# A selective scan hands its finished groups over through ScalarE, GpSimd and TensorE, and two expert layers expand their first pair of slots earlier

## The reference, cut to what matters

```python
x = L0_attn_a_hidden
x = x + _L0_attn_a_ref(_layernorm(x, axis=-1), ...)   # state space layer, 4 heads
x = x + _L0_ffn_ref(_layernorm(x, axis=-1), ...)      # 16 experts, top 1, and a shared one
x = x + _L0_attn_b_ref(_layernorm(x, axis=-1), ...)   # the selective scan
x = x + _L0_ffn_ref(_layernorm(x, axis=-1), ...)      # the experts again

# _L0_attn_b_ref: D_INNER = 256, D_STATE = 16
def step(h, inp):
    dt_t, u_t, B_t, C_t = inp
    dA = jnp.exp(dt_t[..., None] * A)
    h = dA * h + (dt_t * u_t)[..., None] * B_t[:, None, :]
    y_t = jnp.einsum('bds,bs->bd', h, C_t)
    return (h, y_t)
y = y + u_c * D
y = y * jax.nn.silu(z)
out = jnp.einsum('bld,ed->ble', y, W_out)
```

## Time and profile before

| | |
|---|---|
| time, median of 3 runs | 578.69 us (577.18 to 580.83) |
| the profiled execution's own time | 577.94 us |
| its span, first to last instruction | 576.6 us |
| TensorE's mean granted clock | 0.928 of full |
| busy: PE / PEld / DVE / ACT / POOL | 475.7 / 272.6 / 424.5 / 308.6 / 311.1 us |
| instructions | 7377 |
| scan, first L1284 to last L1290 | 247.7 to 488.8 us |
| experts' first transpose, t = 0 and t = 1 | 179.6 and 517.5 us |

### The profile page before, as it was taken

How to read it: one execution, slowest core, us unless ns; L and a number is a source line. 1 busy time by engine, 2 the same in 40 slices (tenths; PEclk the granted TensorE clock), 3 DMA queues, 4 the chain that set the end, 5 groups by cost and what they waited for, 6 DMA issues and landing times.

```text
span 576.6 us, 7377 instructions
## 1 busy us (share of the span) xinstructions
PE 475.7 (82%) x2096; PEld 272.6 (47%) x2096; DVE 424.5 (74%) x865; ACT 308.6 (54%) x598; POOL 311.1 (54%) x292
## 2 busy tenths in 40 slices
PE   0994878899878999898888988797588676899995
PEld 0742445566546985362233433243234231459973
DVE  4278967586652425599999899999999999563333
ACT  2564366464462644567667765875475542444521
POOL 1029743252552226256788668895889566331155
PEclk9997898697978999989998998988988998988999
DMA  8999930000004421355565453555554451024323
GB/s 303 398 331 323 327 109 1 1 2 20 23 33 133 121 78 42 79 151 138 161 152 144 131 134 116 152 174 136 146 148 126 148 152 28 19 63 121 107 69 91
DMA packets 39992, 73.95 MB, mean 128 GB/s; under 512 B 4368, under 2 KB 20240, under 8 KB 39184
## 3 DMA queue, kind: packets, MB, share of 16 engines
q1 hardware_dynamic: 35024, 66.74, 38.7%
q0 software_dynamic: 2048, 4.20, 2.6%
q10 hardware_dynamic: 2880, 2.55, 1.4%
HBM read 66.00 MB, written 26.28 MB: 160 GB/s over the span
## 4 chain that ended last, share of the span: by engine, by line
PE 35%; DVE 28%; issue 17%; ACT 9%; POOL 6%; DMA 3%; ACTq 2%; SPq 0%; DVEq 0%; POOLq 0%
DVE arena L1290 11%; PE psum L677 6%; PE psum L729 5%; PE psum L857 4%; DVE psum L1284 3%; POOL arena L1847 2%; PE psum L741 2%; POOL arena L1801 2%; ACT L1370 2%; PE psum L776 2%; DVE stats L928 2%; PE psum L507 1%; PE psum L855 1%; PE psum L690 1%; DMA x<-x_in 1%
## 5 line engine op out<-in xcount | busy, mean ns | idle before, releaser
L1847 POOL TENSOR_TENSOR arena<-arena 128x512 f32<-128x512 f32 x127 | 158.2, 1271 | 63.8 <-DVE arena L1290 63.6
L857 PE MATMUL psum<-arena,w 128*128 128x512 f32 x256 | 139.1, 655 | 31.1 <-POOL arena L1847 28.5
L1290 DVE TENSOR_TENSOR_SCAN arena<-arena,psum 128x512 f32<-128x512 f32 x128 | 148.4, 1199 | 2.7 <-issue 2.7
L1667 ACT ACTIVATE arena<-arena 128x510 f32<-128x510 f32 x128 | 87.7, 714 | 51.4 <-DVE arena L1290 49.1
L857 PEld LDWEIGHTS psum<-arena,w 128*128 128x128 f32 x256 | 45.3, 200 | 109.9 <-POOL arena L1847 88.8
L1284 DVE TENSOR_TENSOR psum<-psum,arena 128x512 f32<-128x512 f32 x128 | 81.4, 680 | 0.1
L1732 POOL TENSOR_TENSOR arena<-arena 128x512 f32<-128x512 f32 x16 | 20.3, 1266 | 76.1 <-DVE arena L989 76.1
L677 PE MATMUL psum<-xnt,w 128*128 128x512 f32 x128 | 61.3, 628 | 0.0
L1801 POOL DMA_INDIRECT arena<-by_expert,routes x32 | 30.8, 963 | 35.6 <-DMA by_expert<-arena 20.0
L1370 ACT ACT_TABLE_LOAD x27 | 34.6, 1283 | 9.1 <-DMA c<-c_in 8.6
L1764 POOL DMA_INDIRECT by_expert<-xn,routes x32 | 32.0, 1000 | 13.5 <-issue 7.6
(11 more groups left out here) (188 smaller groups left out, 806.7 us busy)
## 6 DMA issues: line engine op xcount, KB each, us to landing
arena<-bc_store SPq DMA_DIRECT2D x64, 512.0 KB, 4.8
by_expert<-w_in SPq DMA_DIRECT2D x4, 4096.0 KB, 44.3
w<-w_in SPq DMA_DIRECT2D x1, 4427.5 KB, 13.2
arena<-by_expert SPq DMA_DIRECT2D x54, 64.0 KB, 1.9
by_expert<-arena SPq DMA_DIRECT2D x52, 64.0 KB, 1.6
by_expert<-w_in SPq DMA_DIRECT2D x1, 1984.0 KB, 67.8
x<-x_in SPq DMA_DIRECT2D x4, 256.0 KB, 7.4
out<-x SPq DMA_DIRECT2D x4, 256.0 KB, 2.7
```

What stands on the lines that cost most here:

```text
L857: nc.tensor.matmul(bank(6 + c), ident, state[c][s % 3], start=False, stop=(n == DS - 1)).then_inc(*summed.inc((s, c)))
L1290: nc.vector.tensor_tensor_scan(state[c][s % 3], decay_b[c][s % 2], bank(2 + c), 0.0, ALU.mult, ALU.add).then_inc(*state_ready.inc((s, c)))
L1667: nc.scalar.activation(live, seq, ACT.Exp, scale=a_neg[:, DS * c + n:DS * c + n + 1]).then_inc(*decay_ready.inc((s, c)))
L1847: nc.gpsimd.tensor_tensor(state[c][s % 3], state[c][s % 3], bc_row[s % len(bc_row)][:, 1, :], ALU.mult).then_inc(*y_done.inc((s, c)))
```

## The change

It has three parts; nothing that is computed changes.

1. For the groups g = 0, 1, 2 ScalarE copies both sums out of the banks in step 16 g + 17 ("sums", into the part of `dtu` that this group no longer needs; signal `sums_taken`), and GpSimd multiplies them by the gate in steps +1 and +2, one half each. `add_up` of the next group's first step now waits for `sums_taken`.
2. For these groups TensorE puts x into the bank of `project_out` by a matmul with the identity, ahead of the projection, so that ScalarE's plain copy of that bank (step +5, "add") is the new x. VectorE's measuring moves from step +5 to +6, root and scale from +6 to +7. Group 3 is closed on VectorE as before (`gate_last`, `close_last`).
3. In both expert layers `expand(0)` and `gate_slots(0)` stand ahead of turning slots 4 to 7.

```diff
@@ due_in_steps
-            what = {0: ["gate"], 4: ["project_out"], 5: ["add"], 6: ["root"], 8: ["turn"], 9: ["logits"],
+            what = {0: ["sums"], 1: ["gate 0"], 2: ["gate 1"], 4: ["project_out"], 5: ["add"], 6: ["measure"], 7: ["root"], 8: ["turn"], 9: ["logits"],
@@ experts, TensorE (ScalarE alike, with gate_slots and take_slots)
                 for k in range(n_pairs + 2):
+                    if k == 0:
+                        expand(0)
                     if k % 2 == 0 and 2 * k + GB < NSLOT:
                         turn_in(2 * k + GB)
-                    if k < n_pairs:
+                    if 0 < k < n_pairs:
                         expand(k)
@@ add_up
-                            pe.wait_ge(*(gated_b[g - 1, c] if g else shared_added[0, NGRP - 1]))
+                            pe.wait_ge(*(sums_taken[g - 1, c] if g else shared_added[0, NGRP - 1]))
@@ project_out
+                    inner = g < NGRP - 1
+                    if inner:
+                        nc.tensor.matmul(b, ident, x_cols[:, group(g)], start=True, stop=True, skip_group_check=True)
@@ VectorE's loop over the steps
-                        if what == "gate":
-                            gate_sums(g)
-                        elif what == "add":
-                            add_b(g)
+                        if what == "measure":
+                            dve.wait_ge(*added_b[g])
+                            measure(3, g)
@@ ScalarE's loop over the steps
-                        if what == "root":
+                        if what == "sums":
+                            for c in range(NCH):
+                                act.wait_ge(*summed[DS * (g + 1) - 1, c])
+                                nc.scalar.activation(dtu[:, c, group(g)], bank(6 + c), ACT.Copy).then_inc(*sums_taken.inc((g, c)))
+                        elif what == "add":
+                            act.wait_ge(*out_b_made[g])
+                            nc.scalar.activation(x_cols[:, group(g)], out_bank[1, g], ACT.Copy).then_inc(*added_b.inc(g))
+                        elif what == "root":
@@ GpSimd's loop over the steps
-                    if what == "place":
+                    if what in ("gate 0", "gate 1"):
+                        c = ("gate 0", "gate 1").index(what)
+                        pool.wait_ge(*zb_ready[g])
+                        pool.wait_ge(*sums_taken[g, c])
+                        nc.gpsimd.tensor_tensor(z[:, c, group(g)], dtu[:, c, group(g)], z[:, c, group(g)], ALU.mult).then_inc(*gated_b.inc((g, c)))
+                    elif what == "place":
```

42 lines of the change are left out of this document (24 added, 18 removed).

## The result

| | before | changed |
|---|---|---|
| time, median of 22 runs each | 577.46 us (574.33 to 581.54) | 581.2 us (576.33 to 583.23) |
| ratio | | 1.0051, 95% interval 1.0030 to 1.0072 |
| scan, first drive product to last recurrence, profiled execution | 241.1 us | 248.2 us |
| experts, first turn to third expansion, t = 0 and t = 1 | 7.54 and 7.07 us | 4.83 and 4.52 us |

What follows compares the result with a forecast made beforehand. VectorE was taken to set the scan's pace and TensorE the experts'. Scan +4.7 and experts -5.1 gave -0.4 us on the median of 578.69, so 578.3 us, range 573.8 to 582.5.

Steps and rivals of the forecast that it cites:

- the scan's term: Scan: late copies at the hand-overs cost more than VectorE's saved work; groups 0 to 2 sum to +4.7 us, low end +1.0.
- the experts' term: Both expert layers: first expansion moved into the DMA wait and TensorE's clock kept up, -5.1 us.
- pile-up in TensorE's queue: Rival, scan: TensorE's lateness makes VectorE wait again at step 23; 581.1 us, or 583.8 in full; chance 0.10.
- Group 0, forecast +3.4: First hand-over: copies behind Silu and table load delay step 19's recurrence by 4.0, less 0.66 for the addition; low end +1.5.
- Group 1, forecast +2.0: Second hand-over: late copies delay step 35's second recurrence by 2.7 us, less 0.66 for the addition; low +0.2.
- 3.4 then 1.9: Hand-overs of groups 0 and 1: half 0 summed 3.4 us after the opening matmul, half 1 1.9 us later.
- the low end of 1.0: Scan's sum if TensorE runs at full rate at the hand-overs: 1.5 + 0.2 - 0.7 = +1.0 us.
- Group 2, forecast -0.7: Third hand-over: the gate's saving is lost to a larger stall in step 53; only the addition's gain is left.
- Hidden hand-over: Rival, scan: the hand-over is hidden, so VectorE's full saving counts; -6.2 us there, total 567.4; chance 0.07.
- TensorE keeps the full clock: Rival, scan hand-overs: no slow matmuls behind the pauses; scan +1.0 us, total 574.6; chance 0.12.
- the clock falls at the experts' start: Rival, experts: TensorE's clock drops despite the shorter pauses; experts only -1.8 us, total 581.6; chance 0.16.
- within 1% as forecast: Whole kernel: no difference beyond about 1% (5.8 us), chance 0.85; faster by more 0.09, slower by more 0.06.

Runs made afterwards that it cites:

- the scan's parts alone: The changed kernel without its experts' part (parts 1 and 2 of the change alone), against the kernel before: 583.89 us, ratio 1.0101.
- The kernel with TensorE kept busy: The changed kernel plus five, six and three unread matmuls while TensorE waits for the copies of groups 0, 1 and 2: 576.01 us, ratio 0.9956 to before.
- the kernel with all gates on VectorE and the later preparations: The changed kernel without part 1, with group 2's u, Silu, rows, dt and group 3's second gate half prepared later: 570.40 us, ratio 0.9844 to before.
- the experts' part alone: The kernel before with only the first pair expanded ahead of turning slots 4 to 7: 574.83 us, ratio 0.9932 to before.
- the last version: The changed kernel with early copies, later preparations and GpSimd products, and projection with what follows one step later: 572.54 us, ratio 0.9888 to before.

## Why the prediction was wrong

**The sum.** -0.4 was 4.7 - 5.1. From the rows of three profiles the scan's term is +7.1 to +8.1, from all profiles the experts' term is -4.5 by its starts and -4.1 by its ends: together +2.6 to +4.0, and measured were +2.9 (1.7 to 4.2). The mechanism of each term was right; the scan's size was not, +4.7 where +7.1 was measured. That the time still lies inside the range is no merit of the sum: the range's upper part had been left open for a pile-up in TensorE's queue and for slow starts of the experts, and the scan's larger loss came from neither.

**Group 0, forecast +3.4: right.** Its stalls are 7.18 us against 1.56 before, less 1.97 us of work that left VectorE (a third of 3.9 and 2.0): +3.65. The pause was 5.05 us where I had 5, and the recurrences came 3.8 and 5.5 us after the opening matmul, where I had 3.4 and 5.3. In the five profiles with this hand-over as in the changed kernel the stalls are 7.2 to 8.8 us (8.5 and 8.8 with groups 1 and 2 on VectorE), so +3.4 lies at the low end of what it costs.

**Group 1, forecast +2.0: this is the step that failed.** 5.39 us of stalls less 1.97 is +3.42. Opening and copies were placed right: VectorE is 1.99 us earlier here than before (its recurrence at 369.25 against 371.24), so TensorE's 376.20 is 378.19 in the old frame, and I had 378.05. But I took "3.4 then 1.9" for the halves, the slow value for the first pair only. The two recurrences were released 3.9 and 6.7 us after the opening: the slow stretch went on through both halves (granted clock 0.50 from 376.20 to 379.78 and on to 381.48). I had worked from the row of the same place, where the second pair was already faster. The second profile of the changed kernel and that of the scan's parts alone have the same pause of 6.76 us, the same slow second half, and stalls of 5.6 us. The kernel with TensorE kept busy shows that it is the clock: 1.82 us from opening to opening at this place, and 4.3 us of the scan's 7.1 come back. My forecast had the clock's share at 3.7 (4.7 less the low end of 1.0), nearly that. What is left over without it is 2.8 where the low end said 1.0: by the stalls of the three groups +2.9, +0.5 and -1.9 (+1.5, +0.2 and -0.7 forecast; the first has the 1.0 us of later copies in it), and 1.2 outside these stalls. The 1.18 us that VectorE waits for the decays of step 34 add nothing to the loss, since right behind them it waits for the sums in any case.

The length of the slow stretch doesn't follow the pause, though. With the copies early in group 0 alone, the pause at the second hand-over was 6.88 us, and the clock was back at 1.00 for the second half:

```profile
375.89 2.08 PE L859 MATMUL psum<-arena 128*128 128x512 f32 x2 [6.88 <-ACT arena L1699]
377.76 1.75 PE L861 MATMUL psum<-arena,w 128*128 128x512 f32 x2
379.35 1.02 PE L859 MATMUL psum<-arena 128*128 128x512 f32 x2
```

With group 2 on VectorE it was 6.89 us and the same (3.26 us to the second opening, then the full rate). There group 1's stalls are 4.1 and 3.9 us, +2.1 and +1.9 with the work that left VectorE: my forecast of +2.0. In the kernel with all gates on VectorE and the later preparations, a pause of 3.14 us at this place was followed by two slow halves (3.58 us to the second opening, which then took 1.92 us for its two records). So the step that failed is the length of the slow stretch. In the changed kernel's two profiles it covered both halves, and what sets its length stays open.

**Group 2, forecast -0.7: off by 0.7.** 3.03 us of stalls against 1.10, less 1.97, is 0.0. The part on the gate was right (gated on VectorE again, no difference that can be told), and so was the larger stall in step 53, 1.74 us. What I had not seen are the stalls of 0.80 and 0.49 us ahead of it. The pair at the third hand-over took 3.23 us from opening to opening (437.11 to 440.34), in the kernel before 2.24, as TensorE's timeline of before shows:

```profile
434.37 1.13 PE L855 MATMUL psum<-arena 128*128 128x512 f32 x2 [3.95 <-DVE arena L1303]
435.34 1.48 PE L857 MATMUL psum<-arena,w 128*128 128x512 f32 x2
436.61 1.91 PE L855 MATMUL psum<-arena 128*128 128x512 f32 x2
```

In the kernel with all gates on VectorE it was 3.57, with a stall of 0.58, so this is not the copies' doing alone: TensorE pauses at this place with either order (3.95 us before, 4.09 changed, 3.79 with all gates on VectorE), and how much of the pair then runs slow differs.

**The experts, forecast -5.1: right in its rows, a little high in the mean.** First turn to third expansion 4.83 and 4.52 us, where I had 4.5 for t = 1, instead of 7.54 and 7.07; the clock stayed at 1.00. The clock falls all the same in 5 of 24 starts, and at t = 1 not all of the gain reaches the end; with both it is about -4.1.

**The rivals.** "Hidden hand-over" (-6.2 in the scan) and "TensorE keeps the full clock" are excluded by the rows; "the clock falls at the experts' start" holds at one start in five; the pile-up in TensorE's queue did not happen: behind step 20 there is no stall until step 34, and VectorE's wait for L861 is all in the groups' first steps. The ratio of +0.5% is within 1% as forecast, but by a sum that was 3.3 us off, 2.4 us of it in the three terms of the scan as the first profile has them, 0.6 to 1.0 in the experts.

**What the forecast of signs would have needed.** The trace of before had pauses of 3.26 and 3.95 us at two hand-overs, and the slow stretches behind them lay differently: from the first matmul on, and from the second pair on. One of them was taken for all. A second half at the slow rate had to be in the range of each group, as a case of its own. With the measured 3.9 and 2.8 us in place of 3.4 and 1.9, group 1 comes to +3.4; with no gain in group 2 the scan's sum is +6.8 and the forecast 578.69 + 6.8 - 5.1 = 580.4. That is hindsight; nothing in the trace of before tells which of the lengths comes.

The Trainium skill (TensorE: Matmul & The Clock Gate, HAM oscillation) describes this case in general, that waits inside a loop drop the clock and the work behind them pays, and advises a loop order without such waits. The trace agrees with the advice: the same work without the first pause, early copies for group 0, is 3.8 us faster. The Trainium skill (ScalarE: Activation LUTs, What ACT_TABLE_LOAD costs) adds a drain of about 1380 ns to a switch of tables; here again it isn't seen: the load at 311.72 is followed by the copies at 313.02, 1.30 us from start to start.

## What to carry to other kernels

Before a product is taken from the engine that sets the pace, walk the queue of the engine that gets it, at the very step: a copy of 0.6 us behind a Silu and two table loads cost more than the 2 us that it saved, and the same copy ahead of them brought the scan back to its old length. A pause of TensorE can cost twice, by its length and by the slow matmuls behind it, and in a forecast the slow stretch needs a range of lengths, not the one that a single row shows; if the pause can't be removed, matmuls that nothing reads can fill it, as they did here. And when an account of stalls shows what an engine waits for (idle time more, busy time less, sum), use it on the trace of before with the change laid over it, per group and both halves.

## What the runs showed of the hardware

- The slow stretch behind a pause differs in length, and the pause's own length doesn't tell it. After 6.76 us (three profiles) it held through both halves, 3.58 us instead of 1.82 from one bank's opening to the next, and the second half still at a granted clock of 0.50; after 6.88 and 6.89 us it held for the first half alone (3.46 and 3.26 us), after 5.05 us too in the changed kernel (3.51 us, then 1.02 us for two records), and after 3.14 us it held through both.
- Matmuls that nothing reads, run during the wait, kept the clock at 1.00: 1.82 us from opening to opening, 5.5 us of the kernel's time.
- Starts of the experts with two short pauses close to each other (0.23 to 1.04 us and 1.08 to 1.30 us) had the lower clock behind them in 5 of 12 cases, those with one of 1.11 to 1.55 us alone in 0 of 12. Which starts lose it differs from kernel to kernel at the same place, which may be part of why the times of one kernel scatter by several us (569.7 to 577.9 with the experts' part alone).
- A wait for a DMA can be another engine's lateness: the rows of B and C landed 4.7 to 5.1 us after their issue, and the issue waited for GpSimd's products of four steps before (1.52 us of VectorE's time in the last version).
